# A selective-scan block with its feed-forward layer: decays from PSUM to a ring in SBUF, single-row loads in rings, another split of the products and another order

## The reference

```python
xz = jnp.einsum('btd,pd->btp', x, W_xproj)
dt_raw, Bm, Cm = xz[..., :64], xz[..., 64:80], xz[..., 80:]
dt = jax.nn.softplus(jnp.einsum('btr,dr->btd', dt_raw, W_dt) + b_dt)
A = -jnp.exp(A_log)
dA = jnp.exp(dt[..., None] * A)                      # the decays
dBx = dt[..., None] * Bm[:, :, None, :] * x[..., None]
def step(h, inp):
    dA_t, dBx_t, C_t = inp
    h = dA_t * h + dBx_t
    return (h, jnp.einsum('bds,bs->bd', h, C_t))
...
x = _layernorm(x + ys + Dp * x)
h = jax.nn.silu(x @ wg.T) * (x @ wu.T)               # wg, wu, wd: int weights / 127
x = _layernorm(x + h @ wd.T)
```

## Time and profile before

| | us |
|---|---|
| median of the runs | 2022.29 |
| profiled execution | 2022.87 |
| its span, first to last instruction | 2021.1 |
| VectorE busy | 1869.1 |
| GpSimd busy | 1768.4 |
| TensorE busy (matmul) | 1729.2 |
| ScalarE busy | 1474.9 |

### The profile page before, as it was taken

The page is one execution under the profiler, slowest core; times in us unless marked ns, Lnnn a source line. Parts: engine busy times, 40 slices in busy tenths (PEclk is TensorE's granted clock), DMA queues, the critical chain, the costliest instruction groups (busy, mean ns, idle before and its releaser), DMA issues.

```text
span 2021.1 us, 35597 instructions
## 1 busy us (share of the span) xinstructions
PE 1729.2 (86%) x10664; PEld 1339.9 (66%) x10664; DVE 1869.1 (92%) x2317; ACT 1474.9 (73%) x2668; POOL 1768.4 (87%) x811
## 2 busy tenths in 40 slices
PE   5688888888889888889888889888889888889887
PEld 3566676666677666777666776666766666766665
DVE  5899999999999999999999999999999999999993
ACT  6767777777777778777677877777777778776752
POOL 5998889988988988988988899989889989889970
PEclk7899999999999999999999999999999999999989
DMA  7234333233333233333234233234233243232300
GB/s 248 95 98 137 104 119 116 86 123 135 105 117 115 83 126 131 105 105 125 89 126 130 96 110 120 100 126 131 95 110 113 96 136 121 99 115 88 112 12 21
DMA packets 102675, 223.18 MB, mean 110 GB/s; under 512 B 9617, under 2 KB 44018, under 8 KB 102642
## 3 DMA queue, kind: packets, MB, share of 16 engines
q1 hardware_dynamic: 102642, 222.78, 33.3%
HBM read 203.87 MB, written 18.87 MB: 110 GB/s over the span
## 4 chain that ended last, share of the span: by engine, by line
PE 49%; issue 15%; ACT 14%; DVE 13%; POOL 7%; DVEq 1%; ACTq 0%; POOLq 0%; DMA 0%; SPq 0%
PE p_o L997 16%; PE p_y L960 13%; PE p_m L984 6%; POOL h L416 5%; DVE h L707 4%; DVE hid L743 3%; DVE h L699 3%; ACT p_da L533 3%; PE p_m L908 3%; PE p_c L937 3%; PE p_m L900 3%; ACT da_k L533 2%; ACT res_n L576 2%; PE p_da L928 2%; DVE silu_g L737 2%
## 5 line engine op out<-in xcount | busy, mean ns | idle before, releaser
L406 POOL TENSOR_TENSOR ub<-u,b_bc 128x1024 f32<-128x1024 f32 x384 | 906.1, 2375 | 0.1
L416 POOL TENSOR_TENSOR h<-h,c_bc 128x1024 f32<-128x1024 f32 x320 | 757.0, 2378 | 0.0
L533 ACT ACTIVATE p_da<-dt,neg_a 128x512 f32<-128x512 f32 x768 | 524.1, 686 | 231.2 <-DVE h L699 229.2
L960 PE MATMUL p_y<-ident,h 128*128 128x128 f32 x4096 | 566.2, 290 | 36.9 <-POOL h L416 36.7
L960 PEld LDWEIGHTS p_y<-ident,h 128*128 128x128 f32 x4096 | 509.7, 150 | 87.0 <-POOL h L416 52.0
L699 DVE TENSOR_TENSOR_SCAN h<-p_da,h_carry,ub 128x512 f32<-128x512 f32 x384 | 474.5, 1266 | 9.2 <-ACT p_da L533 8.3
L699 DVE TENSOR_TENSOR_SCAN h<-p_da,ub 128x512 f32<-128x512 f32 x384 | 452.4, 1208 | 15.0 <-ACT p_da L533 9.3
L997 PE MATMUL p_o<-wt_down,hid 128*128 128x256 f32 x1536 | 352.3, 379 | 3.0 <-DVE res L750 1.6
L997 PEld LDWEIGHTS p_o<-wt_down,hid 128*128 128x128 f32 x1536 | 284.4, 190 | 52.2 <-issue 14.7
L984 PE MATMUL p_m<-x_t,wt_up 128*128 128x512 f16 x744 | 194.3, 384 | 81.1 <-DVE hid L743 81.1
L707 DVE TENSOR_TENSOR h<-h,p_c 128x1024 f32<-128x1024 f32 x192 | 229.9, 1197 | 25.3 <-PE p_c L937 25.3
(11 more groups left out here) (101 smaller groups left out, 1875.7 us busy)
## 6 DMA issues: line engine op xcount, KB each, us to landing
b_bc<-bc_rows_dram SPq DMA_DIRECT2D x128, 768.0 KB, 4.0
c_bc<-bc_rows_dram SPq DMA_DIRECT2D x320, 256.0 KB, 4.2
x_in<-in_L_attn_x SPq DMA_DIRECT2D x32, 512.0 KB, 3.5
out_x<-res_n SPq DMA_DIRECT2D x32, 512.0 KB, 3.0
bc_rows_dram<-bc_rows SPq DMA_DIRECT2D x32, 64.0 KB, 1.6
hid<-in_L_ffn_w_gate SPq DMA_DIRECT2D x1, 768.0 KB, 4.9
hid<-in_L_ffn_w_up SPq DMA_DIRECT2D x1, 768.0 KB, 6.8
res<-in_L_ffn_w_down SPq DMA_DIRECT2D x1, 384.0 KB, 7.2
```

Of the source, the lines that this page charges most:

```text
L406: nc.gpsimd.tensor_tensor(ub[:, i % UB_SLOTS, :, :], u[:, par, :, :], b_bc[:, i:i + 1, :].broadcast_to([P, DH, T]), ALU.mult).then_inc(s_u ...
L416: nc.gpsimd.tensor_tensor(h[:, s % H_SLOTS, :, :], h[:, s % H_SLOTS, :, :], c_bc[:, i:i + 1, :].broadcast_to([P, DH, T]), ALU.mult).then_i ...
L533: nc.scalar.activation(da, dt[:, par, q, :], ACT.Exp, scale=neg_a[:, q, s:s + 1]).then_inc(s_da, 1)
L960: ins = nc.tensor.matmul(p_y_tok[:, k, q * P:(q + 1) * P], h[:, s % H_SLOTS, q, k * P:(k + 1) * P], ident[:, :], start=False, stop=(s == S ...
```

## The change

All decays go to SBUF, into a ring `da` of four slots, and are made three states ahead. The former p_da is now p_ub and holds only transposed u*B. `K_STATES` grows to six, so GpSimd makes u*B of ten states. `POOL_STATES` grows to twelve, so VectorE makes four C products. B rows are loaded one by one into five slots, C rows into six slots, each slot used twice a chunk, and the list of SyncE is written anew. ub has five slots instead of six. The table `AT` is another one, and halves of a transposed state stand earlier in TensorE's slot.

```diff
-POOL_STATES = (0, 1, 2, 3, 4, 7, 8, 9, 10, 11)
-UB_AHEAD = 4
-DA_AHEAD = 1
+POOL_STATES = (0, 1, 2, 4, 5, 7, 9, 10, 11, 12, 13, 14)
+UB_AHEAD = 3
+DA_AHEAD = 3
+DA_SLOTS = 4
...
-    "gate_up": (9, 1), "tanh": (9, 0), "silu": (10, 0), "hidden": (10, 1),
+    "gate_up": (9, 2), "tanh": (9, 1), "silu": (10, 0), "hidden": (10, 0),
...
-K_STATES = (3, 7, 11, 15)
+K_STATES = (2, 7, 8, 9, 13, 15)
 K_AHEAD = 2
 K_SLOTS = 2
-GROUP = 4
-UB_SLOTS = 6
+UB_SLOTS = 5
+B_SLOTS = 5
+C_SLOTS = 6
...
-        b_bc = sb("b_bc", [P, NB, T], F32)
-        c_bc = sb("c_bc", [P, NP, T], F32)
+        b_bc = sb("b_bc", [P, B_SLOTS, T], F32)
+        c_bc = sb("c_bc", [P, C_SLOTS, T], F32)
...
-        da_k = sb("da_k", [P, K_SLOTS, DH, T], F32)
+        da = sb("da", [P, DA_SLOTS, DH, T], F32)
...
+            def broadcast_b(c, j, par):
+                if j >= B_SLOTS:
+                    sp.wait_ge(s_ub, NB * c + (j - B_SLOTS + 1))
+                elif not (isinstance(c, int) and c == 0):
+                    wait(sp, s_ub, NB * (c - 1) + (j - B_SLOTS + NB + 1))
+                s = B_STATES[j]
+                sp.dma_start(b_bc[:, j % B_SLOTS:j % B_SLOTS + 1, :], bc_dram[par:par + 1, s:s + 1, :].broadcast_to(
+                    [P, 1, T])).then_inc(s_b[j % B_SLOTS], 16)
...
                 if last:
                     store(c - 2)
                 if nxt:
-                    broadcast_b(c + 1, 3, 1 - par)
                     broadcast_c(c + 1, 2, 1 - par)
+                    broadcast_c(c + 1, 3, 1 - par)
+                    broadcast_b(c + 1, 5, 1 - par)
+                    broadcast_b(c + 1, 6, 1 - par)
+                    broadcast_c(c + 1, 4, 1 - par)
...
             def decay(c, s, par, q):
                 act.wait_ge(s_dt, c + 1)
-                if s in K_STATES:
-                    i = K_STATES.index(s)
-                    if i >= K_SLOTS:
-                        wait(act, s_scan, 2 * units(c, K_STATES[i - K_SLOTS]))
-                    else:
-                        wait(act, s_scan, 2 * units(c - 1, K_STATES[i - K_SLOTS + NK]))
-                    da = da_k[:, i % K_SLOTS, q, :]
-                else:
-                    wait(act, s_scan, 2 * units(c, s) - 2 + q - 1)
-                    da = p_da[:, q, :]
-                nc.scalar.activation(da, dt[:, par, q, :], ACT.Exp, scale=neg_a[:, q, s:s + 1]).then_inc(s_da, 1)
+                wait(act, s_scan, 2 * (units(c, s) - DA_SLOTS) - 1 + q)
+                nc.scalar.activation(da[:, s % DA_SLOTS, q, :], dt[:, par, q, :], ACT.Exp,
+                                     scale=neg_a[:, q, s:s + 1]).then_inc(s_da, 1)
...
-                    da, dbx = da_k[:, K_STATES.index(s) % K_SLOTS, q, :], p_da[:, q, :]
+                    dbx = p_ub[:, q, :]
...
-                    da, dbx = p_da[:, q, :], ub[:, i % UB_SLOTS, q, :]
+                    dbx = ub[:, i % UB_SLOTS, q, :]
...
-                wait(pe, s_scan, 2 * units(c, s) - 2 + q - 1)
+                if i > 0:
+                    wait(pe, s_scan, 2 * units(c, K_STATES[i - 1]) - 1 + q)
+                else:
+                    wait(pe, s_scan, 2 * units(c - 1, K_STATES[-1]) - 1 + q)
```

More of the change, by code:

```diff
@@ L75, in mamba_ffn_block @@
     NB = N - NK
-    B_GROUP = NB // NK
-    assert K_STATES == tuple(range(GROUP - 1, N, GROUP)) and B_GROUP == GROUP - 1
-    assert NB % UB_SLOTS == N % H_SLOTS == NK % K_SLOTS == 0
+    assert NB % UB_SLOTS == N % H_SLOTS == NK % K_SLOTS == N % DA_SLOTS == 0
+    assert NB == 2 * B_SLOTS and NP == 2 * C_SLOTS and K_STATES[0] > 0
     sum_at = {s: s + SUM_LAG[s in POOL_STATES] for s in range(N)}
     SUM_ORDER = sorted(range(N), key=lambda s: (sum_at[s], s))
-    assert all(sum_at[s] < N or s not in POOL_STATES for s in range(N))
+    assert N - 1 not in POOL_STATES
     x_chunks = x.rearrange("b (h k p) d -> (b h) p k d", p=P, k=TT)
@@ L153, in mamba_ffn_block @@
         bc_dram = nc.dram_tensor("bc_rows_dram", (2, BC, T), F32, kind="Internal").ap()
-        p_da = ps("p_da", [P, DH, T])
+        p_ub = ps("p_ub", [P, DH, T])
         p_y = ps("p_y", [P, DH, T])
@@ L162, in mamba_ffn_block @@
         p_m = ps("p_m", [P, 2, T])
-        tail_ps = (p_m, p_da)
+        tail_ps = (p_m, p_ub)
         tail_t = (tanh_g[:, :], ub[:, 0, 0, :])
@@ L199, in mamba_ffn_block @@
         s_rows_dram = sem("s_rows_dram")
-        s_b = [sem(f"s_b{k}") for k in range(N // GROUP)]
+        s_rows_kept = sem("s_rows_kept")
+        s_b = [sem(f"s_b{j}") for j in range(B_SLOTS)]
         s_ut_ps = sem("s_ut_ps")
@@ L209, in mamba_ffn_block @@
         s_c_ps = sem("s_c_ps")
-        s_c = [sem(f"s_c{i}") for i in range(NP)]
+        s_c = [sem(f"s_c{i}") for i in range(C_SLOTS)]
         s_hc_dve = sem("s_hc_dve")
@@ new lines, in broadcast_c @@
+            def broadcast_c(c, i, par):
+                if i >= C_SLOTS:
+                    sp.wait_ge(s_hc_pool, NP * c + (i - C_SLOTS + 1))
+                elif not (isinstance(c, int) and c == 0):
+                    wait(sp, s_hc_pool, NP * (c - 1) + (i - C_SLOTS + NP + 1))
+                s = N + POOL_STATES[i]
+                sp.dma_start(c_bc[:, i % C_SLOTS:i % C_SLOTS + 1, :], bc_dram[par:par + 1, s:s + 1, :].broadcast_to(
+                    [P, 1, T])).then_inc(s_c[i % C_SLOTS], 16)
@@ new lines, in _ @@
+            rows_out(0, 0)
+            for i in range(B_SLOTS):
+                broadcast_b(0, i, 0)
+                broadcast_c(0, i, 0)
+            broadcast_b(0, 5, 0)
+            broadcast_b(0, 6, 0)
+            def step(c, par, batch, nxt, core, prev, last):
+                if core:
+                    broadcast_c(c, 5, par)
+                    broadcast_b(c, 7, par)
+                    broadcast_b(c, 8, par)
+                    broadcast_c(c, 6, par)
+                    broadcast_b(c, 9, par)
+                    broadcast_c(c, 7, par)
@@ L493, in bc_out @@
                 act.wait_ge(s_proj_ps, c + 1)
-                wait(act, s_rows_dram, 16 * c)
+                wait(act, s_rows_kept, c)
                 wait(act, s_ones, 3)
@@ L593, in _ @@
                 u_out(0, a)
+            for s in range(1, DA_AHEAD):
+                for q in range(DH):
+                    decay(0, s, 0, q)
             act.wait_ge(s_const, 1)
```

62 lines of the change are left out of this document (27 added, 35 removed), and 12 rows, old and new, of the table AT.

## The result

The changed kernel takes 2745.07 us (median of 4 runs, 2742.59 to 2746.45) against 2023.52 for the kernel before, run beside it. That is 1.357 times as long, 95% interval 1.354 to 1.359. The forecast was 1944, and the time lies outside the range of 1900 to 2400. The rival of the whole shared path had said 2593 at least, and 2700 to 2900 where the engines also wait for each other's results.

The account below looks back on a forecast made before the run. VectorE was taken to set the pace, 58.2 us of work in a 60.8 us chunk. Work 56.15 plus idle 2.1 gave 58.3, saving 2.5 us x 31 = 78: 1944 us by the median, own range 1900 to 1995, overall 1900 to 2400.

Parts of the forecast that it names:

- The rival of the whole shared path: Scans of ten states and GpSimd products exclude each other: GpSimd's path 79.2, VectorE 79.4 us a chunk; chance 0.20.
- Decays in a ring of four SBUF slots: 20 scans a chunk read both operands from SBUF: 0.15 us at the low end, 24 on top of GpSimd's 55.2 at the high.
- the rule that it quotes: Trainium skill: a VectorE instruction with two SBUF inputs contends with a GpSimd instruction that reads SBUF; no size given.
- Two C products leave VectorE: VectorE makes four C products a chunk instead of six: 2.2 us less, work from 58.2 to 56.0.
- ScalarE 49.5, TensorE 53.8: Two more token-route states add 3.6 us a chunk to ScalarE and 1.1 to TensorE; neither reaches VectorE's 56.
- ScalarE's wait of 0.40 goes: ScalarE no longer waits for scans to free p_da, so VectorE's 0.40 us a chunk of waiting for decays goes.
- Tiles in a new order, 0.6 left: Hidden directly after silu, a scan and C product before silu: of VectorE's 1.08 us tanh wait a chunk, 0.6 stays.
- Handovers, 0.3 for the transposed u*B and 0.42 for p_c: VectorE's waits on TensorE: 0.3 of 0.43 us a chunk stays for transposed u*B, 0.42 of 0.63 for p_c.
- GpSimd level, 0.8: GpSimd delivers u*B just on time for four states; VectorE idles 0.8 us a chunk for late ub, between 0 and 2.5.
- The sum, 58.3 us a chunk: VectorE work 56.15 plus idle 2.1 us, against 60.8 a chunk: 78 us saved over 31 chunks; forecast chance 0.55.
- In part: Rival: scans and GpSimd products both slow a little and interleave; 2220 us if GpSimd loses half of 24; chance 0.17.
- TensorE never bound: Rival that TensorE binds: 59.3 us a chunk, or 60.8 (2021 us, nothing won) if its C-product wait grows; chance 0.08.

Follow-up runs that it names:

- a_shift8: The complete changed kernel plus eight one-column memsets on VectorE ahead of its loop: 2682.44 us, ratio 1.326.
- m_shift8: The changed kernel with GpSimd's 23 products a chunk replaced by memsets, plus eight one-column memsets ahead of VectorE's loop: 1932.71 us, ratio 0.956.
- b_hid: The kernel before with only the hidden product moved directly behind silu: 2088.38 us, ratio 1.032.
- micro: A separate probe program, not a kernel variant: phases pairing VectorE instructions of one form with GpSimd instructions of one form; no total time given.
- p_shift8: The changed kernel with ten states' decays back in PSUM, transposes at their old places, eight memsets ahead of VectorE's loop: 2218.19 us, ratio 1.097.

## Why the prediction was wrong

The account of the 722 us, by medians: 62.6 are the pause at the loop's turn (`a_shift8`). 749.7 are the shared path, from 2682.44 to 1932.71. The rest of the change gives 90.8 back. The middle term may be somewhat high, and the last with it, since the memsets take GpSimd 51.65 us a chunk where the products would take 55.2.

- *Decays in a ring of four SBUF slots.* This is the step that failed. It priced the scans with two SBUF operands at the low end, 0.15 us a chunk, since "the rows with one operand in each memory are the nearest". The high end was 24 us, a chunk of 79.2 or more. Measured: 81.7 (`a_shift8`), and in the kernel after these scans are 672 us longer over the run, 21 us a chunk. The choice of the low end was wrong, and the step had been told so by the rule that it quotes; by that rule the chances of 0.55 and 0.20 were the wrong way round. The nearest row was near in everything but the one property that was new.
- *Two C products leave VectorE.* Right: 56.0 forecast, 56.08 in `m_shift8`.
- *ScalarE 49.5, TensorE 53.8.* ScalarE 48.9, right. TensorE 52.65, 1.1 less. Neither binds.
- *ScalarE's wait of 0.40 goes.* Right: no row of it is left in the kernel after.
- *Tiles in a new order, 0.6 left.* 5.8 us over 28 chunks in `m_shift8`, 0.2 left. Better than forecast, though in the old order the move of hid alone loses 3% (`b_hid`). Whether the moved gate matmuls and tanh, the transposes or the C products make the difference was not separated. The step also put the place behind silu at nothing. In `m_shift8` hid has 21.0 us of idle time before it, 0.7 a chunk:

```profile
L776 DVE SCALAR_TENSOR_TENSOR hid<-p_m,silu_g 128x512 f32<-128x512 f32 x186 | 128.7, 692 | 21.0 <-DVE silu_g L770 3.1
```

- *Handovers, 0.3 for the transposed u*B and 0.42 for p_c.* 26.5 us, 0.95 a chunk for u*B, and nothing for p_c. The sum of 0.72 was 0.2 too low.
- *GpSimd level, 0.8.* Not shown: with memsets GpSimd has 3.5 us a chunk less to do and waits 185.8 us before rstd in 29 places, about 6.4 a chunk. Taking the 3.5 off leaves some 2.9, the 2 or 3 us that the prediction named. No late ub is in the waits, but that was with the lighter load.
- *The sum, 58.3 us a chunk.* 58.2 between the third and the 31st chunk of `m_shift8`, and 1932.71 us against 1944. The work is right (56.08). The idle time agrees partly by luck: forecast 2.1, measured 2.1, but the 0.8 for a late ub is not in it, and 0.7 before hid is, which no term had. This is the kernel without the shared path and without the pause, with GpSimd's load somewhat lighter; no run with GpSimd's real products came near 1944.
- *Missing term.* Nothing in the prediction spoke of the place of the code. It was worth 62.6 us. What could have been seen: the page of before has an instruction queue with 17 packets, all at the start and the end, and the diff changes the number of VectorE's instructions ahead of the loop. Where the borders lie can't be read from it.
- *Rivals.* The whole shared path was right in mechanism and sign. That 2745 lies in its 2700 to 2900 is luck in part, since 62.6 us of it are the pause: without it the time is 2682, above its 2593 at least. Of its two sums, the one for VectorE holds: 79.4 us a chunk, and two chunks of `a_shift8` have 78.8 busy. The one that fills GpSimd's path doesn't, since GpSimd is busy only 64.4 of 81.7 there. "In part" would have needed instructions that interleave; scans and two-input products don't. TensorE never bound.

## What to carry to other kernels

Before an operand moves from PSUM to SBUF, count for every VectorE instruction how many inputs come from SBUF, and ask what GpSimd reads meanwhile. A form that no row shows isn't priced by its nearest neighbour when a rule names just the property that differs. An engine's pause behind a loop's branch, with a releaser that changes from turn to turn, is looked up in the instruction queue's packets, and tried by moving the loop.

## What was not expected of the hardware

- Scans and two-input products take strict turns: a scan of 1.2 us waits for the product to end and ends 1.08 us after it. At sustained overlap a scan takes 3.29 us and a product 3.25 (`micro`). A wait of this kind stands in no wait row, and a group's mean hides it when only some of its instructions meet the other engine. Beside a one-input GpSimd instruction two scans pass per turn.
- A copy from SBUF to SBUF on VectorE (L135 of `micro`) is drawn into the turns although it has one input: it takes 2.82 us beside a GpSimd product and 0.68 alone. The product took 2.78 us beside it.
- A small product of 128x64 on GpSimd leaves the scans at 1267 ns, against 1201. But it takes turns too, one for one: 1.23 us for each of the 12 beside the scans, 0.31 alone (L85 of `micro`, whose mean of 497 ns mixes them).
- Four instructions fewer ahead of VectorE's loop cost the kernel after 62.6 us, and in a kernel with slack at that place (`p_shift8`) the same shift was worth nothing.
